# First pass of a gated state-space decoder layer: ninth unit before the first heads, tenth behind them, an earlier fifth convolution, GpSimd held off the first sum

## The chip, the cores and the metric

The kernel runs on one core of one Trainium2 chip. The metric is the device time of one execution in microseconds (us), lower is better. A core has a tensor engine (PE, TensorE), a vector engine (DVE), a scalar engine (ACT), GpSimd (POOL) and a queue of transfers issued by SyncE (SP).

## The reference, cut to what matters

For 32 sequences of 64 tokens with 512 features the layer adds three blocks to x. The first, in which the change lies, is a state-space block with 128 heads of 64, in 8 groups:

```python
proj = layernorm(x) @ in_proj_w.T              # gate, x, B, C and step sizes
xBC = silu(causal_conv4(xBC) + conv_b)
dt = clip(softplus(dt + dt_bias), 0)
cum = cumsum(dt * A)                           # within a chunk
scores = (C . B) * exp(cum_i - cum_j) * dt     # lower triangle
y = scores @ x + states carried over + D * x
g = y * silu(gate); g = g * rsqrt(mean(g*g) + eps) * norm_w   # per group
x = x + g @ out_w.T
```

Cross-attention to a context and a mixture of low-rank experts follow; the change does not touch them.

## The kernel before, in words

The tokens are cut into 4 blocks of 512, each worked in 8 passes, one for a group of heads: 32 passes. A pass has 18 **units**, `unit(k)`: products of a 128-column slice of the input weights with the normalised tokens. To keep fp32 accuracy each weight and token is split in a high and a low part, so a unit is 12 matmuls of 512 columns. Units 0 and 1 are B and C; then unit 2+2c is the x slice c and unit 3+2c the gate slice c. B, C and the x slices go through a convolution: ACT makes the first tap from the bank (`tap0(m)`), DVE adds three (`conv(m)`, 2+c for slice c), and ACT applies `silu(m)`. PE turns slice c to token-major (`to_tokens(c)`, "transposes(c)" below), and DVE scales it with the step sizes (`x_tokens(c)`, which also reads `dts`, copied from `dtk`). `heads(c)` multiplies slices c and c+1 with `decay`; DVE adds the skip (`skipped`), multiplies with the gate (`gated`), ACT and POOL split the result (`g_high`, `g_low`), and `project(c)` multiplies it with the output weights into four output banks `p_out` that stay open for a whole pass.

`decay` comes from the running sum of the step sizes: DVE computes softplus as a series (`softplus`) and the sum; it goes through memory, SP loads it as rows, POOL subtracts (`differences`), DVE clamps, ACT exponentiates, DVE multiplies with `cbt` (`decayed`). In the first pass block 0 goes in halves (`clamped_half`, `exp_half`, `decayed_half`).

Weights come raw from memory (`raw_w`, 5 buffers; `raw_o`, 2). For each, ACT makes the high part (`split_w`, `split_o`), and POOL (`w_low`) or DVE (`o_low`) the low part; SP then reloads the raw buffer and stores the split weights for later blocks. Rings of 6 (`w_ring`) and 4 (`o_ring`) hold the split ones. SP works in a fixed order; in the first pass, behind `split_out(0, 0)`, it waits for `o_low(0, 1)` before it issues `raw_o(3)`, the store of that slice, `raw_w(15)` and so on:

```python
def split_out(g, c):
    sp.wait_ge(olo_done, CPG * g + c + 1)
    if c + RAW_O < CPG:
        raw_out(g, c + RAW_O)
```

ACT's order at the end of its turn k=3 in the first pass is `split_o(0,2)`, `split_o(0,3)`, `split_w(0,12)` to `split_w(0,15)`, then `tap0(6)`.

Each engine's order is written out by hand as one program; semaphores alone tie them. Two PSUM banks (`p_in`) take units and transposes; in the first pass units 2 to 5 and 7 use the output banks, which are still free.

Of the kernel before, what the change touches and what calls it, by code (L numbers as in the profile page):

```python
# [15 lines left out]
TB = 512  # L16
# [22 lines left out]
def decoder_kernel(nc, x, ctxv, amask, wt, wdt, owt, params, dtb, alog, ffa, ffb,  # L39
# [10 lines left out]
    with outer:  # L50
# [184 lines left out]
        FIRST_STEPS = 19  # L235
# [30 lines left out]
        def in_bank(k, n):  # L266

            if first(n) and (2 <= k < 6 or k == 7):
                return p_out[1 if k == 7 else k - 2][:, :]
            return p_in[k % 2][:, :]  # L270
# [212 lines left out]
        def _(pe):  # L483
# [39 lines left out]
            unread(4, TB)  # L523
# [9 lines left out]
            def unit(k, tb, g, n):  # L533
# [11 lines left out]
                elif first(n) and k == 7:  # L545
                    pe.wait_ge(gate_done, 1)
# [33 lines left out]
            def to_tokens(c, n):  # L580
                if first(n) and c == 1:
                    pe.wait_ge(xtok_done, 1)
# [223 lines left out]
            def project(c, tb, n, tiles=range(QT)):  # L806

                if tiles[0] == 0:
# [5 lines left out]
                    if c == 0:  # L814
                        pe.wait_ge(*((gate_done, 3) if first(n) else (acc_done, n)))
# [16 lines left out]
            def body(tb, g):  # L832
# [25 lines left out]
                else:  # L858
# [8 lines left out]
                    to_tokens(1, n)  # L867

                for k in range(2, CPG):
# [4 lines left out]
                    if begun or k > 2:  # L874
                        unit(3 + 2 * k, tb, g, n)
                    else:
                        unit(8, tb, g, n)
# [95 lines left out]
        def _(act):  # L973
# [58 lines left out]
            for k in range(FIRST_SPLITS):  # L1032
                split_w(0, k)
            act.wait_ge(wdl_done, 1)
# [65 lines left out]
            def body(tb, g):  # L1100
# [36 lines left out]
                else:  # L1137
# [9 lines left out]
                    tap0(2, n)  # L1147
                    silu(1, n)
                    tap0(3, n)
                    split_w(0, 8, 3)  # L1150
                    silu(2, n)
                    silu(3, n)
                    exp_half(0)

                for k in range(1 if begun else 2, CPG):
                    if begun or k != 3:
                        tap0(2 + k, n)
# [4 lines left out]
                    if k == 2 and not begun:  # L1162
                        split_w(0, 9, 4)
                        refill_o(0)
# [3 lines left out]
                    if k % 2 == 0:  # L1168
                        silu(2 + k, n)
                        gate(k, n)  # L1170
# [16 lines left out]
                    if k == 2 and not begun:  # L1187
                        tap0(5, n)
                        refill(1)
# [157 lines left out]
        def _(dve):  # L1347
# [64 lines left out]
            for q in range(QT):  # L1412
                normal(q, first_tiles[q], acb[:, 0, q, :], None)
            for q in range(QT):
# [11 lines left out]
            def softplus(b, parts):  # L1426

                half = (slice(0, TB // 2), slice(TB // 2, TB))
                for part in parts:
                    if part == 0:  # L1430
# [3 lines left out]
                        link(V.tensor_scalar(cum[:, :], d_e[:, :], 2.0, None, ALU.add))  # L1434
                    if part in (1, 2):
# [130 lines left out]
            skips(0, 0)  # L1566
            softplus(0, (*range(16), 17, 18))
# [189 lines left out]
            def body(tb, g):  # L1757
# [27 lines left out]
                if not begun:  # L1785
                    conv(3, n)
                products(n)
# [14 lines left out]
                else:  # L1802
                    x_tokens(1, n)
                    dve.wait_ge(cbt_done, 1)
                    decayed_half(0)

                dve.wait_ge(dpar_done, n + 1)
                for k in range(1 if begun else 2, CPG):
                    if k == 3 and not begun:
                        normal(QT, xt[:, :], xt[:, :], QT)  # L1810
                    if begun or k != 3:
# [11 lines left out]
                    if k == 3 and not begun:  # L1823
                        decayed_half(1)
                    if k == 3 and begun:
                        decayed(1, n)
                    x_tokens(k, n)
                    if k == 5 and not begun:
                        decayed(1, n)
                    if k == 2 and not begun:  # L1830
                        late(0, tb, g)
                        refill_o(0)
                        conv(5, n)
                        clamped_half(1)
                        refill_o(1)
# [13 lines left out]
                    if k in (2, 3):  # L1849
                        spread(k, tb, g)  # L1850
                    if k == 3:
# [60 lines left out]
        def _(pool):  # L1912
# [7 lines left out]
            for q in range(0, QT, 2):  # L1920
                pool.wait_ge(var_done, q + 2)
                T(rstd[:, q:q + 2], ve[:, q:q + 2], half_neg[:, q:q + 2], ALU.pow).then_inc(rstd_done, 2)
            pool.wait_ge(wdh_done, 1)
            T(wd[:, 1, :, :].rearrange("p k c -> p (k c)"), d_s[:, :],
              wd[:, 0, :, :].rearrange("p k c -> p (k c)").bitcast(F32), ALU.subtract).then_inc(wdl_done, 1)
# [7 lines left out]
            for k in range(RING_W):  # L1933
                w_low(0, k)
# [59 lines left out]
            def body(tb, g):  # L1994
# [21 lines left out]
                for k in range(1, CPG):  # L2016
                    if k == 1 and begun:
                        differences(tb, g, 1, n)
                    if k == 1 and not begun:
                        w_low(0, 8)  # L2020
                        for half in range(2):
                            differences_half(half)
                        w_low(0, 9)
# [13 lines left out]
                    if k % 2 == 0:  # L2037
                        g_low(k - 2, n)
                        if k == 2 and not begun:
                            deviation(coming(tb, g))  # L2040
                        if k == 2 and tb == 0:
# [114 lines left out]
```

## Time and profile before

| | us |
|---|---|
| median of 3 runs | 2824.02 |
| lowest, highest | 2819.71, 2824.45 |
| the profiled execution | 2827.02 |
| its span | 2825.2 |
| PE, DVE, ACT, POOL busy | 2793.4, 2016.1, 1464.0, 1315.3 |

The profiled execution is one more run, with a record of every instruction; all times in rows below are us from the start of its span. Busy times of engines overlap each other. PE is busy nearly all the time, so where it stands still is what can be gained.

### The profile page before, as it was taken

The page shows a single profiled execution, that of the slowest core. Times are in us where ns is not written, and L with a number is a line of the kernel's source. Part 1 is how long each engine was busy: PE and PEld are TensorE (multiplying, and loading weights), DVE is VectorE, ACT ScalarE, POOL GpSimd, SP SyncE. Part 2 cuts the span into 40 slices and gives each one's busy share as a digit, 9 for nine tenths or more (in the row PEclk, how much of TensorE's full clock was granted, in tenths as well). Part 3 has the DMA queues.
Part 4 walks back from the last instruction along what each step waited for, and adds up shares of the span by engine and source line. Part 5 has one row for each costly group of instructions (what it writes and reads, how often), then busy time and mean ns, then how long its engine had stood idle before and what let it go on. Part 6 is the DMA issues. An engine that isn't in the chain of part 4 may idle for free.

```text
span 2825.2 us, 56341 instructions
## 1 busy us (share of the span) xinstructions
PE 2793.4 (99%) x22190; PEld 2267.1 (80%) x22190; DVE 2016.1 (71%) x3212; ACT 1464.0 (52%) x2206; POOL 1315.3 (47%) x842
## 2 busy tenths in 40 slices
PE   7999999999999999999999999999999999999998
PEld 5888888778788888887888888888888888878886
DVE  7777768887667667677676766677766666666767
ACT  5666666655455545455355454454544445454545
POOL 4767767775343433443334443434434334443334
PEclk9999999999999999999999999999999999999999
DMA  7888777878565565565665565555655656555530
GB/s 246 277 302 297 267 272 258 283 258 294 176 195 184 183 196 170 193 201 176 205 198 182 190 200 169 187 184 187 208 182 190 198 172 207 184 183 187 187 131 31
DMA packets 179508, 578.39 MB, mean 205 GB/s; under 512 B 25264, under 2 KB 31920, under 8 KB 171184
## 3 DMA queue, kind: packets, MB, share of 16 engines
q1 hardware_dynamic: 179248, 574.79, 61.8%
q8 instruction: 179, 2.93, 0.4%
q14 instruction: 81, 0.66, 0.1%
HBM read 460.42 MB, written 114.29 MB: 203 GB/s over the span
## 4 chain that ended last, share of the span: by engine, by line
PE 92%; DVE 5%; ACT 1%; issue 1%; DMA 0%; POOL 0%; SPq 0%; DVEq 0%; ACTq 0%; POOLq 0%
PE p_in L485 54%; PE p_out L485 24%; PE p_y L485 8%; PE p_in L586 4%; DVE cv L1483 1%; PE p_y L724 1%; DVE o_ring L1422 1%; PE p_y L829 0%; DVE t_y L1532 0%; DVE mx L1673 0%; DVE decay L1515 0%; DVE g_f L1544 0%; DVE sc L1660 0%; DVE cum L1444 0%; ACT L975 0%
## 5 line engine op out<-in xcount | busy, mean ns | idle before, releaser
L485 PE MATMUL p_in<-xnb,w_ring 128*128 128x512 f32 x6852 | 1675.8, 397 | 4.5 <-DVE cv L1483 2.0
L485 PEld LDWEIGHTS p_in<-xnb,w_ring 128*128 128x128 f32 x6852 | 1262.8, 189 | 266.5 <-issue 5.7
L1483 DVE SCALAR_TENSOR_TENSOR cv<-p_in,cpar,cv 128x504 f32<-128x504 f32 x954 | 699.9, 734 | 450.3 <-ACT cv L975 426.5
L1938 POOL TENSOR_TENSOR g_lo<-g_f,g_hi 128x512 fp32r<-128x512 f32 x256 | 336.6, 1316 | 1179.2 <-ACT g_hi L975 1179.2
L485 PE MATMUL p_out<-o_ring,g_hi 128*128 128x512 f32 x2048 | 639.3, 393 | 0.5 <-POOL g_lo L1938 0.5
L975 ACT ACTIVATE cv<-p_in,cpar 128x512 f32<-128x512 f32 x318 | 246.7, 776 | 620.4 <-PE p_in L485 584.1
L485 PEld LDWEIGHTS p_out<-o_ring,g_hi 128*128 128x128 f32 x2048 | 380.0, 188 | 78.4 <-issue 0.7
L485 PE MATMUL p_out<-o_ring,g_lo 128*128 128x512 f32 x1024 | 399.9, 390 | 0.0
L1520 DVE TENSOR_TENSOR x_tok<-p_in,dts 128x512 f32<-128x512 f32 x256 | 176.6, 690 | 265.8 <-PE p_in L586 264.4
L975 ACT ACTIVATE x_t<-cv 128x512 f32<-128x512 f32 x256 | 160.8, 628 | 308.2 <-DVE t_y L1532 287.6
L1949 POOL TENSOR_TENSOR ss<-ss,g_sq 128x512 f32<-128x512 f32 x190 | 310.5, 1634 | 7.5
L1991 POOL TENSOR_TENSOR decay<-decay,cumk 128x2048 f32<-128x2048 f32 x63 | 234.8, 3728 | 36.7 <-DMA decay<-cum_scr 35.2
L975 ACT ACT_TABLE_LOAD x183 | 234.8, 1283 | 4.1 <-PEq L2150 0.7
L975 ACT ACTIVATE sg<-p_in 128x512 f32<-128x512 f32 x253 | 148.9, 589 | 167.2 <-PE p_in L485 167.2
L1930 POOL TENSOR_TENSOR w_ring<-raw_w,w_ring 128x512 fp32r<-128x512 f32 x144 | 209.7, 1481 | 48.8 <-ACT w_ring L975 36.1
L485 PEld LDWEIGHTS p_out<-o_ring,g_lo 128*128 128x128 f32 x1024 | 192.6, 188 | 40.9
L1532 DVE SCALAR_TENSOR_TENSOR t_y<-x_t,dpar,p_y 128x256 f32<-128x256 f32 x512 | 211.0, 475 | 1.1 <-PE p_y L485 1.1
L1544 DVE TENSOR_TENSOR g_f<-t_y,sg 128x512 f32<-128x512 f32 x256 | 178.4, 738 | 0.1
L975 ACT ACTIVATE g_hi<-g_f 128x512 fp32r<-128x512 f32 x256 | 159.4, 623 | 31.2 <-DVE g_f L1544 30.6
L485 PEld LDWEIGHTS p_y<-decay,x_tok 64*64 64x64 f32 x8192 | 131.3, 134 | 51.4 <-issue 51.4
L586 PE MATMUL p_in<-id_sb,x_t 128*128 128x128 f32 x1024 | 157.9, 277 | 3.5 <-ACT sg L975 1.7
L485 PE MATMUL p_y<-decay,x_tok 64*64 64x64 f32 x8192 | 148.6, 221 | 6.2 <-DVE decay L1502 2.9
(275 smaller groups left out, 2232.4 us busy)
## 6 DMA issues: line engine op xcount, KB each, us to landing
w_ring<-ws_scr SPq DMA_DIRECT2D x432, 512.0 KB, 3.7
o_ring<-ows_scr SPq DMA_DIRECT2D x192, 512.0 KB, 4.7
ws_scr<-w_ring SPq DMA_DIRECT2D x144, 512.0 KB, 6.0
decay<-cum_scr SPq DMA_DIRECT2D x126, 512.0 KB, 6.7
raw_w<-wt SPq DMA_DIRECT2D x144, 256.0 KB, 5.3
ows_scr<-o_ring SPq DMA_DIRECT2D x64, 512.0 KB, 6.2
raw_o<-owt SPq DMA_DIRECT2D x64, 256.5 KB, 5.6
xt<-x SPq DMA_DIRECT2D x12, 256.0 KB, 8.4
```

The lines of the kernel that those rows point to most:

```text
L485: return nc.tensor.matmul(o, lhsT=l, rhs=r, start=first, stop=last)
L586: ins = nc.tensor.transpose(p_in[1][:, q * P:(q + 1) * P], x_t[:, c % 2, q * P:(q + 1) * P], id_sb[:, :])
L724: ins = nc.tensor.transpose(banks[rl][:, gp * P:(gp + 1) * P], pv, id_sb[:, :])
L975: return nc.scalar.activation(dst, src, func, **kw)
L1483: ins = V.scalar_tensor_tensor(acc[:, :, t:SEQ], src[:, :, 0:SEQ - t], cpar[:, 5 * m + 3 - t:5 * m + 4 - t], acc[:, :, t:SEQ], ALU.mult, A ...
L1520: V.tensor_tensor(x_tok[:, c % 2, :, :].rearrange("p q (h d) -> p q h d", h=2), p_in[1][:, :].rearrange("p (q h d) -> p q h d", q=QT, h=2) ...
L1532: ins = V.scalar_tensor_tensor(t_y[:, c % 2, :].rearrange(by_seq, q=QT, s=2)[:, s], x_t[:, c % 2, :].rearrange(by_seq, q=QT, s=2)[:, s], d ...
L1544: V.tensor_tensor(g_f[:, c % 2, :], t_y[:, c % 2, :], sg[:, (CPG * n + c) % GATES, :], ALU.mult).then_inc(g_done, 1)
L1930: T(w_ring[:, k % RING_W, 1, :, :].rearrange("p k c -> p (k c)"), raw_w[:, (UNITS * g + k) % RAW_W, :], w_ring[:, k % RING_W, 0, :, :].rea ...
L1938: T(g_lo[:, c % 2, :], g_f[:, c % 2, :], g_hi[:, c % 2, :].bitcast(F32), ALU.subtract).then_inc(glo_done, 1)
L1949: T(ss[:, :], a, g_sq[:, c % 2, :], ALU.add).then_inc(ss_done, 1)
L1991: T(decay[:, blk, :, :, :], decay[:, blk, :, :, :], last.unsqueeze(3).broadcast_to([P, 8, QT, SEQ]), ALU.subtract) \
```

## The change

It touches the first pass (and what goes before it) only. Unit 8 moves from behind the first heads to before them, in output bank 3; unit 9, which stood behind transposes(2), takes its old place, in `p_in[0]`. The convolution of x slice 2, `conv(4)`, moves ahead of `products`. As the output bank 3 now holds unit 8, `project(0)` waits for `conv(5)`. The low part of the step-size weights goes from POOL to DVE. POOL waits before its fourth `w_low` until the first sum of softplus is done. `o_low(0)` goes ahead of softplus, and `o_low(1)` behind the low part of the next token tile. ACT's and POOL's splits of weights 8 and 9 and the gate of slice 2 move forward with them; PE has one more dummy matmul (5 instead of 4) at the start.

```diff
-        FIRST_STEPS = 19
+        FIRST_SUM, FIRST_STEPS = 5, 19
+        FIRST_BANKS = {2: 0, 3: 1, 4: 2, 5: 3, 7: 1, 8: 3}
...
-            if first(n) and (2 <= k < 6 or k == 7):
-                return p_out[1 if k == 7 else k - 2][:, :]
-            return p_in[k % 2][:, :]
+            if first(n) and k in FIRST_BANKS:
+                return p_out[FIRST_BANKS[k]][:, :]
+            return p_in[0 if first(n) and k == 9 else k % 2][:, :]
...
-            unread(4, TB)
+            unread(5, TB)
...
-                elif first(n) and k == 7:
-                    pe.wait_ge(gate_done, 1)
+                elif first(n) and k in (7, 8):
+                    pe.wait_ge(gate_done, k - 6)
+                elif first(n) and k == 9:
+                    pe.wait_ge(conv_done, 5)
+                elif first(n) and k == 10:
+                    pe.wait_ge(gate_done, 4)
...
                     if c == 0:
-                        pe.wait_ge(*((gate_done, 3) if first(n) else (acc_done, n)))
+                        pe.wait_ge(*((conv_done, 6) if first(n) else (acc_done, n)))
+                    if c == 0 and first(n):
+                        pe.wait_ge(gate_done, 3)
...
                     to_tokens(1, n)
+                    unit(8, tb, g, n)
...
-                    if begun or k > 2:
+                    if begun or k > 3:
                         unit(3 + 2 * k, tb, g, n)
-                    else:
-                        unit(8, tb, g, n)
+                    elif k == 2:
+                        unit(9, tb, g, n)
...
                 split_w(0, k)
+            split_o(0, 0)
             act.wait_ge(wdl_done, 1)
...
                     tap0(2, n)
+                    split_w(0, 8, 3)
                     silu(1, n)
                     tap0(3, n)
-                    split_w(0, 8, 3)
+                    split_w(0, 9, 4)
                     silu(2, n)
+                    tap0(4, n)
                     silu(3, n)
+                    gate(2, n)
                     exp_half(0)
+                    tap0(5, n)
...
                 normal(q, first_tiles[q], acb[:, 0, q, :], None)
+            dve.wait_ge(wdh_done, 1)
+            V.tensor_tensor(wd[:, 1, :, :].rearrange("p k c -> p (k c)"), d_s[:, :],
+                            wd[:, 0, :, :].rearrange("p k c -> p (k c)").bitcast(F32), ALU.subtract).then_inc(wdl_done, 1)
...
             skips(0, 0)
+            o_low(0, 0)
             softplus(0, (*range(16), 17, 18))
...
                     conv(3, n)
+                    conv(4, n)
                 products(n)
...
                     decayed_half(0)
+                    late(0, tb, g)
...
-                    if k == 3 and not begun:
-                        normal(QT, xt[:, :], xt[:, :], QT)
-                    if begun or k != 3:
+                    if begun or k > 3:
                         conv(2 + k, n)
...
-                    if k == 3 and not begun:
-                        decayed_half(1)
...
                     x_tokens(k, n)
+                    if k == 3 and not begun:
+                        decayed_half(1)
...
                     if k == 2 and not begun:
-                        late(0, tb, g)
-                        refill_o(0)
+                        normal(QT, xt[:, :], xt[:, :], QT)
                         conv(5, n)
                         clamped_half(1)
-                        refill_o(1)
...
+                    if k == 3 and not begun:
+                        refill_o(1)
                     if k == 3:
                         refill_o(k)
...
-            pool.wait_ge(wdh_done, 1)
-            T(wd[:, 1, :, :].rearrange("p k c -> p (k c)"), d_s[:, :],
-              wd[:, 0, :, :].rearrange("p k c -> p (k c)").bitcast(F32), ALU.subtract).then_inc(wdl_done, 1)
...
             for k in range(RING_W):
+                if k == 3:
+                    pool.wait_ge(dve_own, FIRST_SUM)
                 w_low(0, k)
...
                         w_low(0, 8)
+                        w_low(0, 9)
                         for half in range(2):
                             differences_half(half)
-                        w_low(0, 9)
```

On PE in the first pass, from unit 6 to the first projection, before (`p_in0` and `p_out1` are banks; rows of 12 with `w_ring` are units, those with `x_t` the transposes, those with `decay` the heads):

```order
L485 MATMUL p_in0<-xnb0,w_ring 128x512 x12
L485 MATMUL p_y<-c_t,b_t 64x64 x8
L485 MATMUL p_out1<-xnb0,w_ring 128x512 x12
L586 MATMUL p_in1<-id_sb,x_t 128x128 x8
L485 MATMUL p_y<-decay,x_tok 64x64 x32
L485 MATMUL p_in0<-xnb0,w_ring 128x512 x12
L586 MATMUL p_in1<-id_sb,x_t 128x128 x4
L485 MATMUL p_in1<-xnb0,w_ring 128x512 x12
L485 MATMUL p_out0<-o_ring,g_hi 128x512 x2
```

And now, in the changed kernel (its line numbers are a little higher):

```order
L486 MATMUL p_in0<-xnb0,w_ring 128x512 x12
L486 MATMUL p_y<-c_t,b_t 64x64 x8
L486 MATMUL p_out1<-xnb0,w_ring 128x512 x12
L591 MATMUL p_in1<-id_sb,x_t 128x128 x8
L486 MATMUL p_out3<-xnb0,w_ring 128x512 x12
L486 MATMUL p_y<-decay,x_tok 64x64 x32
L486 MATMUL p_in0<-xnb0,w_ring 128x512 x12
L591 MATMUL p_in1<-id_sb,x_t 128x128 x4
L486 MATMUL p_out0<-o_ring,g_hi 128x512 x2
```

Unit 8 stands before the heads, unit 9 behind them, and nothing is left between transposes(2) and the projection.

On DVE, from the low part of the first output weights (`o_ring`, L1422) to that of the third and fourth, before (`cv` is conv(5), `xt` the normalised next tile, `decay` the clamp and the product of the second half, `xnb1` the tile's low part):

```order
L1422 SCALAR_TENSOR_TENSOR o_ring<-raw_o,o_ring 128x512
L1483 SCALAR_TENSOR_TENSOR cv<-p_in0,cpar,cv 128x8x63
L1483 SCALAR_TENSOR_TENSOR cv<-p_in0,cpar,cv 128x8x62
L1483 SCALAR_TENSOR_TENSOR cv<-p_in0,cpar,cv 128x8x61
L1496 TENSOR_SCALAR decay<-decay 128x1024
L1422 SCALAR_TENSOR_TENSOR o_ring<-raw_o,o_ring 128x512
L1388 TENSOR_SCALAR xt<-xt,mv,rstd 128x512
L1502 TENSOR_TENSOR decay<-decay,cbt 128x1024
L1520 TENSOR_TENSOR x_tok<-p_in1,dts 128x512
L1393 TENSOR_TENSOR xnb1<-p_y,xnb1 128x4x128
```

And now, from the next tile's normalisation on:

```order
L1398 TENSOR_SCALAR xt<-xt,mv,rstd 128x512
L1497 SCALAR_TENSOR_TENSOR cv<-p_out3,cpar,cv 128x8x63
L1497 SCALAR_TENSOR_TENSOR cv<-p_out3,cpar,cv 128x8x62
L1497 SCALAR_TENSOR_TENSOR cv<-p_out3,cpar,cv 128x8x61
L1510 TENSOR_SCALAR decay<-decay 128x1024
L1534 TENSOR_TENSOR x_tok<-p_in1,dts 128x512
L1516 TENSOR_TENSOR decay<-decay,cbt 128x1024
L1403 TENSOR_TENSOR xnb1<-p_y,xnb1 128x4x128
L1435 SCALAR_TENSOR_TENSOR o_ring<-raw_o,o_ring 128x512 x3
```

The normalisation is ahead of conv(5), the product of the second half of decay stands behind x_tokens(3), and the low parts of output weights 1, 2 and 3 are in one piece behind the tile's low part.

## Rows read from the trace of the kernel before

**Rows 1.** The page: busy us, share of the span and instructions.

```profile
PE 2793.4 (99%) x22190; PEld 2267.1 (80%) x22190; DVE 2016.1 (71%) x3212; ACT 1464.0 (52%) x2206; POOL 1315.3 (47%) x842
```

**Rows 2.** Stretches: length; busy of PE, PEld, DVE, ACT, POOL; clock, DMA.

```profile
0.00:91.80 91.80, 75.82 (x444) 58.18 (x445) 72.27 (x104) 54.39 (x84) 46.72 (x36) 0.93 0.79 265
91.80:700.00 608.20, 605.58 (x4625) 492.22 (x4626) 470.08 (x658) 370.84 (x577) 424.36 (x261) 1.00 0.81 277
700.00:2750.00 2050.00, 2046.61 (x16383) 1666.50 (x16382) 1414.79 (x2289) 1000.18 (x1468) 812.36 (x510) 1.00 0.58 187
```

**Rows 3.** Timeline of PE, 41 to 73 us: start, duration, what [idle before].

```profile
41.34 3.02 PE L485 MATMUL p_out<-xnb,w_ring 128*128 128x512 f32 x12
49.19 1.16 PE L485 MATMUL p_y<-decay,x_tok 64*64 64x64 f32 x64 [2.89 <-DVE decay L1502]
51.38 5.46 PE L485 MATMUL p_in<-xnb,w_ring 128*128 128x512 f32 x12 [1.02 <-DVE cv L1483]
56.64 0.95 PE L586 MATMUL p_in<-id_sb,x_t 128*128 128x128 f32 x4
66.81 0.63 PE L491 MATMUL p_y<-id_sb,xt 128*128 128x128 f32 x4 [2.63 <-DVE xt L1388]
67.28 0.75 PE L586 MATMUL p_in<-id_sb,x_t 128*128 128x128 f32 x4
67.68 4.54 PE L485 MATMUL p_in<-xnb,w_ring 128*128 128x512 f32 x12
```

**Rows 4.** A stretch of 2 us in unit(8), columns as in rows 2.

```profile
54.00:56.00 2.00, 2.00 (x6) 1.54 (x5) 0.00 (x0) 0.66 (x2) 1.28 (x1) 0.50 1.02 340
```

**Rows 5.** Timeline of DVE, 10 to 26 us.

```profile
10.65 1.49 DVE L1388 TENSOR_SCALAR g_f<-acb,mv,rstd 128x512 f32<-128x512 f32 x1
18.57 1.46 DVE L1434 TENSOR_SCALAR cum<-d_e 128x512 f32<-128x512 f32 x1 [2.49 <-ACT d_e L975]
25.09 0.43 DVE L1442 TENSOR_SCALAR cum<-d_e 128x512 f32<-128x512 f32 x1
```

**Rows 6.** Timeline of DVE and POOL, 42 to 49 us.

```profile
42.86 1.08 DVE L1472 COPY dts<-dtk 128x64 f32<-128x64 f32 x1
44.15 1.93 POOL L1983 TENSOR_TENSOR decay<-decay,cumk 128x1024 f32<-128x1024 f32 x1 [0.25 <-DMA decay<-cum_scr]
44.90 0.69 DVE L1520 TENSOR_TENSOR x_tok<-p_in,dts 128x512 f32<-128x512 f32 x1 [0.95 <-PE p_in L586]
45.50 1.13 DVE L1496 TENSOR_SCALAR decay<-decay 128x1024 f32<-128x1024 f32 x1
47.82 1.23 DVE L1502 TENSOR_TENSOR decay<-decay,cbt 128x1024 f32<-128x1024 f32 x1 [0.59 <-ACT decay L975]
```

**Rows 7.** Timeline of all engines, 63 to 76 us.

```profile
63.49 1.76 DVE L1422 SCALAR_TENSOR_TENSOR o_ring<-raw_o,o_ring 128x512 fp32r<-128x512 f32 x1
66.13 0.43 SPq L295 DMA_DIRECT2D raw_w<-wt  x1
67.87 3.70 POOL L1991 TENSOR_TENSOR decay<-decay,cumk 128x2048 f32<-128x2048 f32 x1 [1.50 <-DVE decay L1502]
68.67 0.68 DVE L1393 TENSOR_TENSOR xnb<-p_y,xnb 128x512 fp32r<-128x512 f32 x1
69.19 2.29 ACT L975 ACTIVATE w_ring<-raw_w 128x512 fp32r<-128x512 f32 x4
69.27 2.85 DVE L1422 SCALAR_TENSOR_TENSOR o_ring<-raw_o,o_ring 128x512 fp32r<-128x512 f32 x1
72.26 0.78 ACT L975 ACTIVATE cv<-p_in,cpar 128x512 f32<-128x512 f32 x1 [0.78 <-PE p_in L485]
73.72 2.26 DVE L1483 SCALAR_TENSOR_TENSOR cv<-p_in,cpar,cv 128x504 f32<-128x504 f32 x3
```

**Rows 8.** DMA issues at 66.14 to 66.5 us: KB each, us to landing.

```profile
raw_w<-wt SPq DMA_DIRECT2D x1, 256.0 KB, 4.7
```

**Rows 9.** Timeline of PE at 91.8 us: heads(4).

```profile
91.77 1.16 PE L485 MATMUL p_y<-decay,x_tok 64*64 64x64 f32 x64 [0.91 <-DVE decay L1515]
```

More of the change, by code:

```diff
@@ L580, in to_tokens @@
             def to_tokens(c, n):
-                if first(n) and c == 1:
-                    pe.wait_ge(xtok_done, 1)
+                if first(n) and c in (1, 3):
+                    pe.wait_ge(xtok_done, c)
                 pe.wait_ge(silu_done, CONVS * n + 3 + c)
@@ L1161, in body @@
                         silu_table()
-                    if k == 2 and not begun:
-                        split_w(0, 9, 4)
-                        refill_o(0)
                     if k == 3 and tb == 0:
@@ L1169, in body @@
                         silu(2 + k, n)
-                        gate(k, n)
+                        if begun or k > 2:
+                            gate(k, n)
                         g_high(k - 2, n)
@@ L1187, in body @@
                     if k == 2 and not begun:
-                        tap0(5, n)
                         refill(1)
@@ L1434, in softplus @@
                         link(V.tensor_scalar(cum[:, :], d_e[:, :], 2.0, None, ALU.add))
+                        assert b or own[0] == FIRST_SUM
                     if part in (1, 2):
@@ L1805, in body @@
                     decayed_half(0)
+                    late(0, tb, g)
                 dve.wait_ge(dpar_done, n + 1)
                 for k in range(1 if begun else 2, CPG):
-                    if k == 3 and not begun:
-                        normal(QT, xt[:, :], xt[:, :], QT)
-                    if begun or k != 3:
+                    if begun or k > 3:
                         conv(2 + k, n)
@@ L1830, in body @@
                     if k == 2 and not begun:
-                        late(0, tb, g)
-                        refill_o(0)
+                        normal(QT, xt[:, :], xt[:, :], QT)
                         conv(5, n)
                         clamped_half(1)
-                        refill_o(1)
                     if k == CPG - 1 and not final(n):
@@ L2037, in body @@
                     if k % 2 == 0:
-                        g_low(k - 2, n)
                         if k == 2 and not begun:
                             deviation(coming(tb, g))
+                        g_low(k - 2, n)
                         if k == 2 and tb == 0:
```

## The prediction, written before the result was known

> **What bounds the kernel now.** I read the page, then the busy time by stretches, then the tensor engine's timeline, then those of the engines it waits for. TensorE is busy 99% of the span [rows 1]. The stretches show where the rest lies: of the first 91.8 us it works 75.82, and from there to 2750 us it is idle 2.6 us in 608 and 3.4 us in 2050 [rows 2]. Behind 91.8 us the kernel is a full queue of matmuls, so what the change is worth is how much earlier or later heads(4) start, at 91.77 us [rows 9]. (I count units, convolutions, heads and projections by the number in the call: unit(8), conv(5).)
>
> In the first pass TensorE's longest stops are 2.89 us before heads(0), with 1.02 before unit(8), and 2.63 before the transposes of the next token tile [rows 3]. Each is followed by a slow unit: twelve matmuls take 3.02 us at 41.34 (2.8 until the next begins), but 5.46 and 4.54 us behind the stops [rows 3]; in such a stretch the granted clock is 0.50, the level of 1.2 GHz [rows 4]. The 16.0 us of idle time up to 91.8 [rows 2] and 4 us lost in slow units are 0.7% of the time; nothing here can be worth more.
>
> **The change, step by step.** Times are us from the span's start, at full clock first; what the clock adds comes at the end.
>
> *Start.* Normalising the third tile took 1.49 us beside a GpSimd subtraction; a like operation alone takes 0.43 [rows 5]. The subtraction now runs on VectorE (about 0.7, as other products of that width). That frees the transposes and ScalarE's copies by 0.8 us. The first sum took 1.46 us beside GpSimd, against the same 0.43 [rows 5]. GpSimd now waits for it, so up to 1.0 more. But o_low(0) now stands before it and falls among GpSimd's own subtractions, so it pushes the third of these into the sum; I count 0.5 of the 1.0. The running sum then ends 1.3 us earlier (bounds 0.8 and 1.8). The extra 512-column dummy matmul ends near 9.1, before the transposes at 10.2: nothing.
>
> *conv(4) sooner.* Three steps, 2.26 us [rows 7], now stand ahead of the copy into dts. 2.26 less 1.3 puts that copy 1 us later, where it meets GpSimd's second half of differences: these too come 1.3 earlier and end about 44.8 (44.15 + 1.93 less 1.3) [rows 6]. Before, the copy was held by the first half until 43.94 [rows 6]; now by the second until 44.85. So x_tok(0) starts at 44.9, as before [rows 6]. Behind it the clamp, 1.13 us beside GpSimd [rows 6], has GpSimd out of its way and takes 0.55 (it ended at 46.63, that long after GpSimd). The first half of decay is ready at 48.5 instead of 47.82 + 1.23 = 49.05 [rows 6].
>
> *unit(8) ahead of heads(0).* It starts behind transposes(1), at 44.9 + 0.69 + 0.5 = 46.1, and takes 2.8: heads(0) start at 48.9, 0.3 earlier than 49.19, and unit(8), which ended at 56.8 [rows 3], is out of the way. Then heads 1.16, unit(9) 2.8, transposes(2) at 52.8 instead of 56.64 [rows 3]. Here the edit gains 3.8 us.
>
> *project(0) behind conv(5).* Unit(8) lies in an output bank, so the projection now waits for conv(5). VectorE: x_tok(2) from 53.4 to 54.05; normal of the next tile, 0.43 to 1.46 by [rows 5], taken as 0.7; conv(5) 2.26: 56.95. TensorE stops 3.7 us, a stop that did not exist. project(0), twelve matmuls again, 2.8; tile transposes 0.6; transposes(3) end at 60.9, before at 68.0. Gain here 7 us.
>
> *o_low(1) behind it all.* This edit decides. x_tok(3) ends at 61.5 and the second half of decay at 62.75 (1.23). In that moment GpSimd is released for the differences of the second block, 3.70 us [rows 7], and runs 62.85 to 66.5. VectorE does low (0.68, with one input in PSUM, unaffected [rows 7]) and comes to o_low(1) at 63.4. The same pair stands in the trace: o_low(2) was begun at 69.27 and took 2.85 us, to 72.12, because the differences ran from 67.87 to 71.57; alone it is 0.7 [rows 7]. So o_low(1) ends at 67.1; before it ended at 65.25 [rows 7], now 1.85 later although all around it is earlier. The Trainium skill (SBUF — State Buffer, Who interferes with whom) has it as a rule: a VectorE instruction with two SBUF inputs and a GpSimd instruction that reads SBUF share a port pair, and the later one is blocked until the first is finished. By that rule the price is the whole rest of the differences, as the row has it; it speaks against placing o_low(1) here.
>
> Queued behind o_low(1): SyncE waits for it before raw_o(3), the store of the second output weights, and then raw_w(15). Before, raw_w(15) was issued at 66.13, 0.88 behind o_low(1), and landed 4.7 us later [rows 7, 8]. Now it is issued at 68.0 and lands at 72.7. ScalarE's four splits (2.29 us from 69.19, ending 71.48 [rows 7]) end with the one that needs it, at 73.3, and tap0(6) stands behind them: it ends at 74.1, before at 73.04. conv(6) starts then; before, it started at 73.72 [rows 7]. So 7 us gained have become 0.4 lost. From conv(6) to heads(4) at 91.77 I see a chain without slack (conv, skipped, gated, ScalarE's copies and splits, o_low(4), conv(7), silu, table, exp, decayed, heads), so heads(4) come at 92.15. TensorE is done with project(1) at 70.2 and stands 8 us: the gain is turned into one long wait.
>
> *The clock.* TensorE now has stops of 4 us (unit(7) and transposes(0), earlier with the rest, end near 41.7, transposes(1) wait for x_tok(0), and unit(8) has to be done before heads(0)), 3.7 (before project(0)) and 8 (before transposes(4)). The rows give, behind stops of 2.6 and 3.9 us, 1.5 and 2.4 us more for the unit [rows 3]. Before, only the 2.4 lay on the chain; it is in the times above, and the new order starts from 48.9 without it. Now unit(8) is on the chain: 1.5 to 2.4, taken 2.0. Project(0): 0.8 to 1.5, since part falls on unit(10), which nobody waits for: 1.2. Unit(12) delays tap0(7), with some 0.8 of cover by ScalarE: 0 to 1.6, taken 0.7. Together 3.9.
>
> **Sum.** 0.4 + 3.9 = 4.3 us later than the profiled execution. That one took 2827.02 us (span 2825.2), 3.0 above the median of the three runs; taking the 3.0 off again, 2824.02 + 4.3 = about 2828 us. 0.2% is 5.6 us, and about what a measurement of this kernel can tell from no change; this is inside.
>
> **Rivals.**
>
> A, *the delayed o_low(1) does not gate* (GpSimd's differences wait for their data, or let VectorE through, or the transfer lands sooner). For it: the o_low at 63.49 took 1.76 us, not 2.85 [rows 7]. Against: the decay rows of the second block were loaded long before. o_low(1) would end at 64.1, raw_w(15) land at 69.7, tap0(6) end at 71.1, conv(6) start 2.6 earlier; with the clock's 3.9, +1.3: 2825 us, and 2821 with none of it. Chance 0.16.
>
> B, *TensorE sets the pace throughout*: the 7 us at transposes(3) carry through to heads(4), less 1 for the clock: 2818 us. For it: every TensorE stop of before is indeed shortened. Against: silu(6) needs conv(6), which needs tap0(6) behind raw_w(15). Chance 0.07.
>
> C, *the clock stays up*: the slow stretch begins some time behind a stop and may miss the units. For it: heads(0), directly behind the 2.89 us stop, took 1.16 us like heads(4) [rows 3, 9]. Against: both units that followed such stops were slow. Then +0.4: 2824.5 us. Chance 0.09.
>
> D, *slower*: one mechanism, the half clock over the whole of unit(8), project(0) and unit(12), which stand directly behind the three stops. By the worst row, 2.4, 2.4 and 1.6 with the 0.4: 6.8 us, 2831 us. It decides from a loss of 5.2 us at the clock. The clock falls in stretches whose place is not tied to the program, so some executions will have it. The Trainium skill (TensorE: Matmul & The Clock Gate, HAM oscillation) says that waits which let the clock fall make the work behind each start cold; twelve matmuls of 512 columns at its cold rate are an estimate of 5.1 us, which would be D. Chance 0.14.
>
> The forecast itself has 0.54, with 2824.5 to 2830.5.
>
> **How the numbers follow.** Slower by over 0.2% is most of D (0.12) and the upper fifth of the forecast (0.11): 0.23. Faster by over 0.2% is B and a tail of A: 0.08. The rest, 0.69, is within. The range that leaves 2 in 10 out goes from A without clock loss, 2821, to a little above D, 2832.5.
>
> **What the profile after would show.** Right, if: the first sum takes 0.43 to 1.0; x_tok(0) is within 0.4 of 44.9; heads(0) come behind unit(8) at 49 to 51; the largest TensorE waits are before project(0) (3 to 4 us, released by conv(5)) and before transposes(4) (6 us or more, released by ScalarE); o_low(1) takes about 3.7 us and ends with the GpSimd differences; tap0(6) starts behind a wait of ScalarE for raw_w; heads(4) start at 92 to 97. Wrong, if o_low(1) takes 0.7, or ScalarE does not wait ahead of tap0(6) (A, B), or the granted clock is 1.00 behind the stops (C). The forecast fails altogether if VectorE is not held where I put it: then everything behind 63 us comes earlier by up to 3 us.

## The result, and the profile after

The changed kernel takes 2832.85 us, the median of ten runs (2828.64 to 2836.15), against 2823.66 us for ten runs of the kernel before (2819.71 to 2829.31). The ratio is 1.0029, with an interval of 1.0020 to 1.0038: slower by 9.2 us by medians and 8.2 by the ratio, about 0.3%. That is 4.9 us above the forecast. By medians it is 0.35 us beyond the upper end of the range, by the ratio (1.0029 times the 2824.02 us of the forecast, 2832.2 us) just inside it; and it is the side (slower by over 0.2%) that had a chance of 0.23. The profiled execution took 2828.64 us, the shortest of the ten, so its trace alone shows only part of the loss.

The stretches of the profiled execution answer to [rows 2]: length, busy time of the engines, granted clock, share and rate of the transfers.

```profile
0.00:91.80 91.80, 72.07 (x433) 55.84 (x434) 65.90 (x103) 50.94 (x79) 44.15 (x35) 0.93 0.76 260
91.80:700.00 608.20, 603.35 (x4615) 490.00 (x4614) 469.70 (x655) 371.43 (x577) 423.76 (x260) 1.00 0.80 275
700.00:2750.00 2050.00, 2046.64 (x16390) 1666.56 (x16390) 1415.37 (x2292) 1001.46 (x1471) 812.36 (x510) 1.00 0.58 188
```

TensorE works 3.75 us less up to 91.8, and 2.2 us less in the stretch up to 700, which is new: the kernel behind 91.8 us is no longer a full queue at once. TensorE's timeline shows where (start, duration, instruction, idle time before it and what ended it); it answers to [rows 3, 9]:

```profile
44.63 1.12 PE L591 MATMUL p_in<-id_sb,x_t 128*128 128x128 f32 x4 [3.91 <-DVE x_tok L1534]
45.40 5.23 PE L486 MATMUL p_out<-xnb,w_ring 128*128 128x512 f32 x12
50.56 1.16 PE L486 MATMUL p_y<-decay,x_tok 64*64 64x64 f32 x64
...
58.85 0.70 PE L486 MATMUL p_out<-o_ring,g_hi 128*128 128x512 f32 x2 [3.75 <-DVE cv L1497]
...
62.12 0.60 PE L591 MATMUL p_in<-id_sb,x_t 128*128 128x128 f32 x4
...
80.26 1.09 PE L591 MATMUL p_in<-id_sb,x_t 128*128 128x128 f32 x4 [8.00 <-ACT sg L983]
81.00 7.29 PE L486 MATMUL p_in<-xnb,w_ring 128*128 128x512 f32 x24
...
95.15 1.16 PE L486 MATMUL p_y<-decay,x_tok 64*64 64x64 f32 x64 [0.92 <-DVE decay L1529]
...
103.42 0.63 PE L591 MATMUL p_in<-id_sb,x_t 128*128 128x128 f32 x4 [1.43 <-ACT sg L983]
103.80 5.70 PE L486 MATMUL p_in<-xnb,w_ring 128*128 128x512 f32 x24
```

In order: transposes(1) behind a stop of 3.91 us; unit(8), 5.23 us; heads(0) at 50.56; project(0) behind a stop of 3.75, released by conv(5) (`cv`); transposes(3) at 62.12, before at 67.28 [rows 3]; then transposes(4) behind a stop of 8.00, and units 12 and 13 in 7.29 us where 5.70 is usual (as the last row has it for two units at full clock). heads(4) start at 95.15, before at 91.77 [rows 9]. Last comes a stop that the kernel before does not have, 1.43 us before transposes(6).

The chain of work that ended last goes, between 65 and 77 us, through the o_low(1) of the prediction (start, duration, what; DMA is the time from issue to landing):

```profile
65.18 3.73 DVE o_ring L1435
68.93 0.33 SPq L299
69.30 0.43 SPq L306
69.78 4.73 DMA raw_w<-wt
...
75.06 0.77 ACT cv L983
75.86 0.75 DVE cv L1497
```

It is the sequence that was forecast: o_low(1), SyncE's raw_o(3), store and raw_w(15), the landing 4.73 us later, a split, tap0(6), conv(6). ScalarE's timeline shows that raw_o(3), issued first, holds it nearly as long: it stands 8.40 us for that load, and then only 0.32 us for raw_w(15):

```profile
71.93 0.72 ACT L983 ACTIVATE o_ring<-raw_o 128x512 fp32r<-128x512 f32 x1 [8.40 <-DMA raw_o<-owt]
...
74.53 0.63 ACT L983 ACTIVATE w_ring<-raw_w 128x512 fp32r<-128x512 f32 x1 [0.32 <-DMA raw_w<-wt]
```

VectorE's timeline has the two places where it is held, and GpSimd's has what holds it:

```profile
64.50 0.68 DVE L1403 TENSOR_TENSOR xnb<-p_y,xnb 128x512 fp32r<-128x512 f32 x1
65.10 4.46 DVE L1435 SCALAR_TENSOR_TENSOR o_ring<-raw_o,o_ring 128x512 fp32r<-128x512 f32 x2
...
94.92 4.18 DVE L1435 SCALAR_TENSOR_TENSOR o_ring<-raw_o,o_ring 128x512 fp32r<-128x512 f32 x1
99.03 2.26 DVE L1497 SCALAR_TENSOR_TENSOR cv<-p_in,cpar,cv 128x504 f32<-128x504 f32 x3
```

```profile
64.66 3.69 POOL L2005 TENSOR_TENSOR decay<-decay,cumk 128x2048 f32<-128x2048 f32 x1 [2.94 <-DVE decay L1516]
...
94.62 3.93 POOL L2005 TENSOR_TENSOR decay<-decay,cumk 128x2048 f32<-128x2048 f32 x1 [4.62 <-DMA decay<-cum_scr]
```

The row at 65.10 is o_low(1) and (2) together: alone they start at 65.10 and 68.82 and take 3.80 and 0.74. low at 64.50, with an input in PSUM, takes its usual 0.68 beside the differences. o_low(5) at 94.92 starts 0.3 us behind the next differences and takes 4.18; in the kernel before it started at 91.54, one us ahead of them (92.58), and took 0.75. (Between the two traces o_low(5) moved by 3.4 us and these differences by 2.0.) So conv(8) and, behind it, transposes(6) are late: that is the 1.43 us stop.

### The profile page after: what moved, and what is told of

Its sections match the earlier page's. It is cut to its first block, busy times and chain, and to the rows that moved or that the text cites. A ratio compares the mean times of both kernels' runs of the same rounds, so it can differ in the third digit from the quotient of the medians.

```text
span 2826.9 us, 56347 instructions
## 1 busy us (share of the span) xinstructions
PE 2789.2 (99%) x22192; PEld 2264.2 (80%) x22192; DVE 2011.0 (71%) x3213; ACT 1463.0 (52%) x2206; POOL 1312.4 (46%) x841
## 4 chain that ended last, share of the span: by engine, by line
PE 91%; DVE 6%; ACT 1%; issue 1%; DMA 0%; SPq 0%; POOL 0%; DVEq 0%; ACTq 0%; POOLq 0%
PE p_in L486 53%; PE p_out L486 24%; PE p_y L486 8%; PE p_in L591 4%; DVE cv L1497 1%; PE p_y L729 1%; DVE o_ring L1435 1%; PE p_y L836 0%; DVE t_y L1546 0%; DVE mx L1688 0%; DVE decay L1529 0%; DVE g_f L1558 0%; DVE cum L1458 0%; DVE sc L1675 0%; ACT cv L983 0%
## 5 line engine op out<-in xcount | busy, mean ns | idle before, releaser
L983 ACT ACTIVATE g_hi<-g_f 128x512 fp32r<-128x512 f32 x256 | 159.3, 623 | 30.8 <-DVE g_f L1558 30.2
L591 PEld LDWEIGHTS p_in<-id_sb,x_t 128*128 128x128 f32 x1024 | 118.5, 141 | 54.5 <-issue 18.7
```

Source lines behind the costliest of these rows:

```text
L591: ins = nc.tensor.transpose(p_in[1][:, q * P:(q + 1) * P], x_t[:, c % 2, q * P:(q + 1) * P], id_sb[:, :])
L983: return nc.scalar.activation(dst, src, func, **kw)
```

## The experiments

All times are medians; ratios are against runs of the kernel before on the same chip, where it had a median between 2822.3 and 2824.3 us. In the cuts of code, lines left out are marked `...`. Where two versions ran on different chips, both the difference of the medians and that of the ratios are given: they differ by up to 2 us, which says how well such a difference is known.

### One step put back: o_low(1) early

```
                        clamped_half(1)
+                       refill_o(1)
...
-                   if k == 3 and not begun:
-                       refill_o(1)
```

> The changed kernel with one step put back: the output weights' o_low(1) directly behind the clamp of the second decay half, where VectorE stands idle from 59.3 to 62.8 us, and no longer behind low at 65.1. Theory (o_low(1), blocked by GpSimd's differences, gates SyncE's two loads): o_low(1) takes about 0.75 us and ends near 60.1, SyncE issues raw_o(3) there and raw_w(15) near 61, the last w_ring split ends near 67 and conv(6) starts near 69 (behind o_low(2), which the differences now hold) against 75.9; transposes(4) start near 73 against 80.3, and the time falls by 5 to 7 us to 2826 to 2828. Rival (TensorE's stops before unit 8 and project(0), and the clock, are the loss): conv(6) comes sooner but the time stays within 1.5 us of 2832.9.

Measured: **2823.61 us**, ratio 1.0004 (0.9995 to 1.0012). The whole loss is gone, 9.2 us by medians and 7.1 by the ratios (1.0029 less 1.0004). That is at or above the upper end of the 5 to 7 expected, and the rival is out. But TensorE's stop before transposes(4) did not go to zero, it fell from 8.00 to 2.66 us. VectorE's timeline:

```profile
58.80 1.76 DVE L1435 SCALAR_TENSOR_TENSOR o_ring<-raw_o,o_ring 128x512 fp32r<-128x512 f32 x1
...
66.40 0.68 DVE L1403 TENSOR_TENSOR xnb<-p_y,xnb 128x512 fp32r<-128x512 f32 x1
67.00 5.50 DVE L1435 SCALAR_TENSOR_TENSOR o_ring<-raw_o,o_ring 128x512 fp32r<-128x512 f32 x2
72.42 2.26 DVE L1497 SCALAR_TENSOR_TENSOR cv<-p_in,cpar,cv 128x504 f32<-128x504 f32 x3
```

o_low(1) ends at 60.56, out of everyone's way. Now o_low(2) and (3), 5.50 us together for what takes 1.40 alone, keep conv(6) until 72.42. Before, it started at 73.72 [rows 7]. So of the 3.3 us by which this execution has transposes(3) earlier (64.02 against 67.28), 1.3 arrive at conv(6). Heads(4) come at 91.39, 3.8 us sooner than in the changed kernel. The rest of the 7.1 to 9.2 us is not in this one trace; the mean granted clock of the runs is higher too (0.9967 against 0.9950), and what that is worth is worked out below.

### The same step alone, in the kernel before

```
                        clamped_half(1)
-                       refill_o(1)
...
                        spread(k, tb, g)
+                   if k == 3 and not begun:
+                       refill_o(1)
```

> The kernel before with only o_low(1) moved behind the low of the next tile, as the change has it. Theory: o_low(1) would run 69.3 to 72.1, under the differences, instead of ending at 65.25; SyncE's raw_w(15) goes out about 7 us later, near 73, and conv(6) starts near 80 against 73.7; the time rises by 5 to 7 us to 2829 to 2831. Rival (that place costs nothing, other parts of the change do): within 1.5 us of the kernel before.

Measured: **2831.85 us**, ratio 1.0029 (1.0017 to 1.0040), 8.2 us slower: nearly all of the change's loss with one of its edits. The rival falls. In VectorE's timeline o_low(1) and (2) take 3.85 us from 67.33, and conv(6) starts at 77.06, waiting for ScalarE's tap0(6) (expected: near 80):

```profile
67.33 3.85 DVE L1422 SCALAR_TENSOR_TENSOR o_ring<-raw_o,o_ring 128x512 fp32r<-128x512 f32 x2
...
77.06 2.27 DVE L1483 SCALAR_TENSOR_TENSOR cv<-p_in,cpar,cv 128x504 f32<-128x504 f32 x3 [1.99 <-ACT cv L975]
```

### The differences wait for o_low(1) and (2)

```
                            pool.wait_ge(s_done, 1)
+                           pool.wait_ge(olo_done, 3)
                            differences(tb, g, 1, n)
```

> The changed kernel with the differences on GpSimd waiting until o_low(1) and o_low(2) are done. Theory (the 3.8 us of o_low(1) are the differences holding it): o_low(1) falls to about 0.75 us, ends near 65.9, raw_w(15) is issued near 66.8 and conv(6) starts near 73 against 75.9, the differences end 1.5 to 2 us later with nobody waiting; time down by 2 to 3 us, to 2830 to 2831. Rival (o_low(1) is slow for another reason, its own access or the stores): it still takes over 3 us and the time stays or rises.

Measured: **2828.81 us**, ratio 1.0017 (1.0008 to 1.0026): 4.0 us less than the change by medians, 3.4 by the ratios. Both o_lows now take 1.40 us together, ending at 66.78: it is the differences that held o_low(1). But conv(6) came at 75.12, not at 73:

```profile
65.38 1.40 DVE L1435 SCALAR_TENSOR_TENSOR o_ring<-raw_o,o_ring 128x512 fp32r<-128x512 f32 x2
72.38 0.75 DVE L1435 SCALAR_TENSOR_TENSOR o_ring<-raw_o,o_ring 128x512 fp32r<-128x512 f32 x1 [5.60 <-ACT o_ring L983]
75.12 1.51 DVE L1497 SCALAR_TENSOR_TENSOR cv<-p_in,cpar,cv 128x504 f32<-128x504 f32 x2 [2.00 <-ACT cv L983]
```

```profile
65.46 0.67 DVE o_ring L1435
...
66.15 5.45 DMA raw_o<-owt
...
75.12 0.75 DVE cv L1497
```

SyncE issued raw_o(3) at 66.15 instead of 68.93, but it landed 5.45 us later; in the changed kernel ScalarE could go on with it at 71.93, 3.0 us after its issue. 2.8 us gained at VectorE were 0.3 at ScalarE. Why this transfer took longer is open. Transposes(4) came 0.7 us sooner (79.53), but heads(4) came at 95.10, against 95.15: on the path of this profiled execution nothing of the gain is left. So this run shows what held o_low(1), and not how freeing it lowered the median. By the slope of time against clock given below, the higher mean clock (0.9962 against 0.9950) is about 2 us of it; the rest is not explained.

### The start part alone, in the kernel before

```
+            V.tensor_tensor(wd[:, 1, ...], d_s[:, :], wd[:, 0, ...], ALU.subtract).then_inc(wdl_done, 1)
...
+            o_low(0, 0)
             softplus(0, (*range(16), 17, 18))
...
             for k in range(RING_W):
+                if k == 3:
+                    pool.wait_ge(dve_own, FIRST_SUM)
                 w_low(0, k)
```

> The kernel before with only the start part of the change: VectorE makes the step sizes' low weights, GpSimd waits for the first sum, o_low(0) ahead of the softplus, one more unread matmul. Theory: the running sum ends 1.3 us sooner (0.8 to 1.8) and the time falls by about that, to 2822 to 2823. Rival: the part loses (the third w_low comes later, units wait) and the time is above 2825.

Measured: **2821.39 us**, ratio 0.9995 (0.9986 to 1.0004): 2.3 us by medians, 1.4 by the ratio, and an interval that holds no change. In the changed kernel's trace, where this part is the same, the first sum took 0.65 us instead of 1.46 and the scan behind it ended at 31.43 instead of 33.91. 0.85 of that is an earlier start (the first transposes at 9.35 and 10.20, behind token tiles that landed earlier), 1.6 the edit.

### Matmuls that nobody reads, in the two stops

```
+            def kept_up(count):
+                for _ in range(count):
+                    mm(p_y[:, 1, :], xnb[0][:, 0, 0, 0:P], xnb[0][:, 0, 0, :], True, True)
...
                     to_tokens(0, n)
+                    kept_up(12)
                     to_tokens(1, n)
...
                     to_tokens(k, n)
+                    if k == 2 and not begun:
+                        pe.wait_ge(yread, 2)
+                        kept_up(12)
```

> The changed kernel (o_low(1) still late) with 12 matmuls whose product nobody reads in TensorE's stop before transposes(1) and unit 8, and 12 more in the stop before project(0). Theory (each stop is paid twice, once as a wait and once as half clock behind it): units 8 and the heads behind it and project(0) run at full clock in every execution, transposes(3) come 2 to 4 us sooner, and since x_tok(3), low and o_low(1) hang on them the time falls by 2 to 4 us, to 2829 to 2831. Rival (the time is set by o_low(1) and SyncE alone, or the added matmuls only get in the way): within 1 us of 2832.9.

Measured: **2829.14 us**, ratio 1.0017 (1.0008 to 1.0026): 3.7 us less than the change by medians, 3.4 by the ratios. Its trace has heads(4) at 92.87, 2.3 us sooner. The stretches of unit(8), of project(0), and of what follows the third stop, which was left as it was:

```profile
44.97:47.92 2.95, 2.95 (x15) 2.16 (x14) 2.44 (x4) 1.06 (x1) 0.00 (x0) 1.00 1.09 421
56.33:59.14 2.81, 2.81 (x12) 2.29 (x13) 0.41 (x1) 2.66 (x3) 2.81 (x2) 1.00 0.49 193
72.80:82.30 9.50, 4.72 (x13) 3.89 (x14) 7.76 (x12) 6.79 (x12) 6.75 (x6) 0.50 1.03 413
```

Both units run at 1.00, 2.95 and 2.81 us. In the changed kernel's profiled execution, what follows the third stop lay in a stretch at 0.50 (the level of 1.2 GHz), and so did unit(8), but project(0) did not (the rows, in this order):

```profile
77.52:84.35 6.83, 4.09 (x12) 3.44 (x13) 5.54 (x10) 4.96 (x9) 4.03 (x3) 0.50 1.03 411
43.39:50.21 6.82, 5.58 (x15) 4.55 (x16) 4.51 (x8) 1.06 (x1) 0.96 (x2) 0.50 1.05 353
56.00:62.00 6.00, 3.15 (x15) 2.63 (x16) 3.25 (x5) 5.53 (x8) 5.72 (x5) 1.00 0.25 99
```

> o1_early with the same 24 unread matmuls. In o1_early's profile unit 8 took 5.29 us at half clock (3.0 at full) and project(0) 5.35 (2.9 at full). Theory: both are given back, x_tok(3) comes at 60 to 62 instead of 64.66, and the time is 2820 to 2821.5, below both kernels. Rival (VectorE, held by the differences at 67.0 to 70.8, sets conv(6), and the differences only move with it): no more than 1 us.

Measured: **2823.08 us**, ratio 0.9998 (0.9989 to 1.0007). That is 0.5 us less than o1_early by medians and 1.7 by the ratios, with intervals that overlap: less than the theory's 2.1 to 3.6, and the rival's "no more than 1" is not excluded. The rival's mechanism is not what the traces show: o_low(2) and (3) are held as before (5.51 us from 62.98), but they moved with the path, and transposes(3), conv(6) and heads(4) all came 4.0 us sooner (60.00, 68.41 and 87.38, against 64.02, 72.42 and 91.39). How much of this is the difference between two executions is open; the mean granted clock rose from 0.9967 to 0.9978.

### conv(5) sooner, and the differences later

```
                    if k == 2 and not begun:
+                       conv(5, n)
                    x_tokens(k, n)
```

> o1_early with conv(5) ahead of x_tok(2) and of the next tile's normalization. Theory: project(0), which waits for conv(5)'s end at 58.15 to get its output bank, starts 1.5 to 2.2 us sooner and so do transposes(3) and all behind them: 2821.5 to 2822.5. Rival (g_low(0) on GpSimd or the clock takes the place of the wait): within 0.7 us of 2823.6.

Measured: **2822.15 us**, ratio 0.9992 (0.9983 to 1.0001): 1.5 us less than o1_early by medians, 3.4 by the ratios. TensorE's stop before project(0) went from 3.74 to 2.04 us, as expected.

> o1_early with the differences on GpSimd waiting for o_low(1), (2) and (3). In o1_early o_low(2) took 3.80 us and conv(6) began at 72.4, behind o_low(3). Theory (VectorE, held by GpSimd, now sets conv(6)): o_low(2) and (3) take 0.75 us each, conv(6) starts near 69, transposes(4) come 2 to 3 us sooner, 2820.5 to 2822. Rival: the differences and the w_low behind them end 1.6 us later and unit 12 waits for its w_low, so that the time stays within 1 us.

(The edit is that of dif_waits with 4 in place of 3.) Measured: **2822.11 us**, ratio 0.9992 (0.9983 to 1.0000). VectorE is no longer held, and conv(6) follows at once:

```profile
67.27 0.68 DVE L1403 TENSOR_TENSOR xnb<-p_y,xnb 128x512 fp32r<-128x512 f32 x1
67.87 1.40 DVE L1435 SCALAR_TENSOR_TENSOR o_ring<-raw_o,o_ring 128x512 fp32r<-128x512 f32 x2
69.70 2.27 DVE L1497 SCALAR_TENSOR_TENSOR cv<-p_in,cpar,cv 128x504 f32<-128x504 f32 x3 [0.42 <-ACT cv L983]
```

From low at 67.27 to conv(6) it takes 2.4 us, in o1_early 6.0. The time followed by 1.5 by medians and 3.4 by the ratios; the intervals of o1_early and of each of these two just overlap.

### Everything together, in both orders

Here the next pass's first differences also wait, for o_low(5):

```
                    if k == 5 and not final(n):
+                       if first(n):
+                           pool.wait_ge(olo_done, 6)
```

> The changed kernel's order with everything together: o_low(1) early, conv(5) ahead of x_tok(2), the 24 unread matmuls, the differences waiting for o_low(1) to (3), and the next pass's first differences waiting for o_low(5), which they held for 4.1 us at 95 in the changed kernel. If the gains were additive to o_low(1)'s 9: 1.5 each for conv(5) and the differences, 0.5 to 3 for the matmuls, 1.4 for the last: 2817 to 2819. Rival (they share one slack, VectorE sets the pace): 2821 to 2822.

Measured: **2821.32 us**, ratio 0.9992 (0.9983 to 1.0001). Transposes(4) start at 70.63 and heads(4) at 84.91, 10.2 us sooner than in the changed kernel and 6.9 sooner than [rows 9]; yet it is only 1.7 us below the kernel before by medians, 2.3 by the ratio. Profiled executions mislead here: that of the kernel before took 3.4 us more than its median, this one 1.3 less. The rival's figure holds.

> all_new_order without the 24 unread matmuls: what the clock still gives once the waits are gone. all_new_order gave 2821.3. If half clock behind the two stops still costs in each execution, 1.5 to 3 us more, 2823 to 2824.5; if the slack behind units 8 and project(0) takes it, within 1 us of 2821.3. Against the kernel before: a gain of 1 to 3 us if the changed order is worth anything once o_low(1) is back in its place.

Measured: **2822.78 us**, ratio 0.9998 (0.9989 to 1.0007): 1.5 us above the same with the matmuls, between the two expectations and not resolved.

> The kernel before with the start part of the change alone and the two waits of GpSimd's differences. start_alone gave 2821.4. Theory (VectorE held by the differences sets the path in the old order too): 1 to 3 us less, 2818.5 to 2820.5. Rival (in the old order conv(6) waits for ACT's tap0, not for VectorE): within 1 us of 2821.4.

Measured: **2822.15 us**, ratio 0.9993 (0.9985 to 1.0002). No gain over start_alone: the rival holds.

```
                    to_tokens(1, n)
+                   kept_up(12)
```

> start_dif_waits with 12 unread matmuls in TensorE's stop between transposes(1) and heads(0). In start_alone the heads took 1.99 and unit 8 3.73 us behind that stop (1.16 and 3.0 at full clock). Theory: both at full clock in each run, 1 to 2.5 us less than start_dif_waits. Rival: the slack behind unit 8 (project(0) had 2.2 us of stop behind it) takes it, no gain.

Measured: **2821.09 us**, ratio 0.9993 (0.9984 to 1.0002): 1.1 us below start_dif_waits by medians, at the lower edge of what was expected, with the same ratio, so within the noise. No version is shown to beat the kernel before.

## Why the prediction was right, and where it failed

The measured time lies at the very end of the range, and the range reached it by its width: a loss of 4.3 us was forecast, 8.2 to 9.2 were measured, and the part from 2824.5 to 2830.5, which had 0.54, does not hold it. The steps in order:

**Start: right.** Forecast: the running sum 1.3 us earlier. Found: 1.6.

**conv(4) and x_tok(0): right.** x_tok(0) came at 43.88. With the 0.85 us by which this execution started earlier, 44.7; the forecast was 44.9.

**unit(8), project(0): right.** Both stops are there, 3.91 and 3.75 us, each released by what was named. Transposes(3) start 5.2 us earlier than before.

**o_low(1): right, up to heads(4) in size too.** The path up to heads(4) was forecast at 91.77 + 4.3 = 96.1; it came at 95.15, or 96.0 with the earlier start. That this agrees to 0.1 us is in part luck: the sum took 2.0 us of clock for unit(8), 1.2 for project(0) and 0.7 for unit(12), and in this execution they were 2.2, nothing and 1.6 (units 12 and 13). o_low(1) took 3.80 us and ended with the differences. The Trainium skill's rule on the shared port pair (SBUF — State Buffer, Who interferes with whom: a VectorE instruction with two SBUF inputs and a GpSimd one that reads SBUF exclude each other) stood behind this: the trace agrees, 3.80 us beside the differences, 0.7 when they wait. What lands last was a close thing: the forecast named raw_w(15), and ScalarE stood 8.40 us for raw_o(3) and 0.32 for raw_w(15).

As to its price, rival A put 3 us on an o_low(1) that is not held (7 with no loss at the clock). The nearest run, dif_waits, gave 3.4 to 4.0, though its one trace has none of that at heads(4). Putting o_low(1) back in its old place is a larger edit and gave 7.1 to 9.2: 3.8 us of it at heads(4) in the traces, and by estimate about 3 by the clock (1.7 thousandths, at the slope below). The gain that was eaten was small in itself: with o_low(1) out of the way, the next two o_lows are held in its place, and conv(6) comes only 1.3 us earlier than before.

**"Behind 91.8 us the kernel is a full queue": this step failed.** The forecast ended its accounting at heads(4). In the kernel before, o_low(5) started one us ahead of the next differences, in the changed one 0.3 behind them. Between heads(4) and the next pass's state products lie 32.4 us in the changed kernel and 30.8 in the one before: 1.6 us that no term held. But it is not shown that the late heads(4) reversed the pair, nor what this costs in the median. o1_early, whose median is that of the kernel before, has the same in its trace, with heads(4) at 91.39 and 32.4 us from there to the state products:

```profile
91.16 4.18 DVE L1435 SCALAR_TENSOR_TENSOR o_ring<-raw_o,o_ring 128x512 fp32r<-128x512 f32 x1
...
90.26 4.53 POOL L2004 TENSOR_TENSOR decay<-decay,cumk 128x2048 f32<-128x2048 f32 x1 [3.70 <-DMA decay<-cum_scr]
...
99.65 0.63 PE L591 MATMUL p_in<-id_sb,x_t 128*128 128x128 f32 x4 [1.44 <-ACT sg L983]
```

No run frees o_low(5) alone.

**The clock: right in the profiled execution, too small for the median.** The forecast took 3.9 us, as the middle of the bounds, and called the full loss (D, 6.4 of clock) a thing of some executions. In the profiled execution unit(8) lost 2.2 us (5.23 against 3.02) and units 12 and 13 1.6, together 3.8, and project(0) nothing. But that was the shortest of ten. The mean granted clock of these ten runs is 0.9950, that of the profiled one 0.997. Each run records one, so the price can be read: over 104 runs of the kernel before (mean 0.9968) the time rises by 1.7 us for each thousandth that the clock falls, over the ten of the changed one by 1.5. Two thousandths are then an estimated 3 to 3.4 us of the 4.2 between profiled run and median. D's 2831 with the 1.6 us above is 2832.6, and the median is 2832.85, but that is an agreement of two sums and shows nothing: the changed kernel's one trace has full clock at project(0), and no trace of it has the whole of D. keep_up supports a larger clock term: 24 matmuls in the first two stops brought the mean clock to 0.9972 and the time down by 3.7 us. The Trainium skill (TensorE: Matmul & The Clock Gate, Wait — 56ns, not 53.3ns?) gives 426.7 ns for a matmul of 512 columns at the cold clock, from which the estimate of 5.1 us for twelve comes; unit(8)'s row has 5.23.

**The loss by cause (an estimate).** By the same slope, 1.8 thousandths of mean clock are 3.1 of the 9.2 us. That leaves 6 for waits. The two traces show 5.0 at the next pass's state products (127.6 against 122.6), or 5.8 with the earlier start, with the same time at half clock up to 91.8 in both (13.6 us, summed from stretches of 2 us). Behind that point the profiled execution of the kernel before took 3.3 us more than the changed one, and so the two end only 1.6 us apart. Part of it is a stretch at half clock that the changed kernel's execution does not have; the stretch from 725 us, before and after:

```profile
725.00:750.00 25.00, 22.85 (x161) 18.58 (x160) 16.13 (x27) 10.63 (x17) 10.38 (x9) 0.93 0.69 219
725.00:750.00 25.00, 22.86 (x170) 18.67 (x169) 19.35 (x31) 14.41 (x22) 10.73 (x8) 1.00 0.59 188
```

**Still open:** why raw_o(3) took 5.45 us in dif_waits; what puts the differences ahead of o_low(5), and its price; in which stretches the changed kernel's slower runs lost their clock; and whether the new order of units itself costs something against start_alone (o1_early 1.0004, start_alone 0.9995, intervals overlap).

## What to carry to other kernels

When a step is moved behind others on VectorE, ask which GpSimd instruction is released at that moment. Here a small operation with both inputs in SBUF (0.74 us alone) that started just behind a long GpSimd one cost the whole of it, 3.80 and 4.18 us, and what waited for it on the DMA queue came as much later. One such line made the whole loss, and the margin of such a pair is best read from both starts (o_low(5): one us in the kernel before). Do not end the sum at the first full queue: look at the next place where two such instructions are close. And compare medians, each run with its granted clock: two profiled executions differed by 1.6 us where the medians differ by 9.2.

## What the runs showed of the hardware that was not expected

- **Granted clock and time move together, run by run.** The 31 runs of the kernel before with a clock of 0.998 took 2821.2 us in the mean, the 25 with 0.997 2822.9, the 37 with 0.996 2825.0, the 8 with 0.995 2826.1. So most of what looks like noise in this kernel goes with the clock. In the profiled executions the half clock lies in the first pass and behind 2750 us, and in some at 725 to 750 us, far from any edit.
- **Twenty-four matmuls whose product nobody reads held the clock at 1.00** through unit(8) and project(0) in the profiled execution; behind the third stop, left empty, TensorE then spent 9.5 us at 0.50 (72.8 to 82.3), longer than any such stretch of the changed kernel (6.8).
- **GpSimd's short subtractions hold VectorE too:** in o1_early o_low(1) took 1.76 us beside a w_low of 1.75, against 0.74 alone.
- **An earlier issue is not an earlier landing:** raw_o(3) issued 2.8 us sooner landed 0.3 us sooner.
